# First-layer weights of an expert slot loaded in two transfers of 4 KB rows instead of one of 8 KB rows

## What is computed

```python
aff = x @ centroids.T
assign = jnp.argmax(aff, axis=1)
...
for e in range(nE):
    h = _layernorm(xs, ln_g[e], ln_b[e])
    h = jax.nn.relu(h @ w1[e].T + b1[e])
    ye = xs + h @ w2[e].T + b2[e]
    y = y + jnp.where((es == e)[:, None], ye, 0.0)
out_sorted = alpha * y + (1.0 - alpha) * xs
```

## The kernel before

| line | what |
|---|---|
| L771, L812 | tensor engine's wait for first weights |
| L780, L816 | layer 1 of a full, of a mixed slot |
| L799, L832 | layer 2 of a full, of a mixed slot |
| L2165 | the transfer that the change splits |

## Time and profile before

### The profile page before, as it was taken

One profiled execution on the slowest core, in us unless ns is written; L12 is line 12 of the kernel. 1 busy time (PEld: TensorE's weight loads), 2 busy tenths in 40 slices (PEclk: granted clock), 3 DMA queues, 4 the chain that ended last, 5 costly groups with the idle time before them and its releaser, 6 DMA issues.

```text
span 830.1 us, 19760 instructions
## 1 busy us (share of the span) xinstructions
PE 809.3 (97%) x7474; PEld 549.3 (66%) x7474; DVE 531.5 (64%) x1515; ACT 342.3 (41%) x574; POOL 281.4 (34%) x393
## 2 busy tenths in 40 slices
PE   8999999999999999999999999999999999999994
PEld 5655475476466557558547636859989976777673
DVE  5564368767757856866787755624579556566572
ACT  2444415513522541641541452232323275657660
POOL 3505011431512413223143160415454545443532
PEclk9999999999999999999999999999999999999998
DMA  7710300220030020040030033324543888978940
GB/s 255 221 49 26 77 1 1 65 66 1 27 103 1 27 53 1 2 128 2 1 97 9 1 103 129 108 66 164 190 148 134 301 318 305 323 268 315 345 201 17
DMA packets 63956, 96.47 MB, mean 116 GB/s; under 512 B 39347, under 2 KB 52276, under 8 KB 55926
## 3 DMA queue, kind: packets, MB, share of 16 engines
q1 hardware_dynamic: 58566, 83.56, 30.1%
q0 software_dynamic: 4864, 11.10, 4.3%
q10 hardware_dynamic: 432, 0.54, 0.2%
HBM read 84.22 MB, written 11.23 MB: 115 GB/s over the span
## 4 chain that ended last, share of the span: by engine, by line
PE 70%; DVE 17%; issue 5%; ACT 5%; POOL 1%; DMA 1%; another core or an unknown queue 0%; DVEq 0%; SPq 0%; ACTq 0%; POOLq 0%
PE ps L678 11%; PE ps L780 10%; PE ps L799 10%; PE ps L672 7%; PE ps L611 6%; PE ps L635 6%; PE ps L816 4%; PE ps L832 4%; DVE w_sb L1162 3%; PE ps L643 3%; PE ps L484 3%; DVE x3x L1162 3%; ACT arena L1662 2%; DVE st_ln L958 2%; DVE arena L1092 2%
## 5 line engine op out<-in xcount | busy, mean ns | idle before, releaser
L678 PE MATMUL ps<-ff2T,hT 128*128 128x256 f32 x512 | 121.6, 385 | 0.2 <-ACT hT L1654 0.2
L672 PE MATMUL ps<-x3x,ff1T 128*128 128x512 f32 x256 | 118.2, 605 | 0.1
L1662 ACT ACTIVATE arena<-ps 128x1536 f32<-128x1536 f32 (+3 forms) x49 | 65.1, 1328 | 113.3 <-DVE arena L1092 113.3
L678 PEld LDWEIGHTS ps<-ff2T,hT 128*128 128x128 f32 x512 | 94.3, 190 | 21.0 <-issue 8.1
L799 PE MATMUL ps<-w_sb,arena 128*128 x400 | 95.6, 382 | 0.0
L1880 POOL TENSOR_TENSOR rs_ln<-mv_ln,eps 128x4 f32<-128x4 f32 x24 | 4.9, 204 | 263.7 <-DVE mv_ln L965 263.7
L672 PEld LDWEIGHTS ps<-x3x,ff1T 128*128 128x128 f32 x256 | 46.0, 189 | 59.0 <-issue 50.9
L799 PEld LDWEIGHTS ps<-w_sb,arena 128*128 128x128 f32 x400 | 72.2, 190 | 12.2 <-issue 4.3
L611 PE MATMUL ps<-arena 32*128 32x512 f32 (+7 forms) x896 | 73.0, 434 | 3.1 <-ACT hT L1111 1.4
L1092 DVE SCALAR_TENSOR_TENSOR arena<-ps,arena 128x512 f32<-128x512 f32 (+4 forms) x59 | 45.0, 771 | 47.8 <-PE ps L635 28.8
L611 PEld LDWEIGHTS ps<-arena 32*128 32x128 f32 x896 | 36.0, 184 | 37.4 <-issue 17.9
(11 more groups left out here) (240 smaller groups left out, 1519.8 us busy)
## 6 DMA issues: line engine op xcount, KB each, us to landing
arena<-in_w SPq DMA_DIRECT2D x27, 1024.0 KB
hT<-in_w SPq DMA_DIRECT2D x16, 1024.0 KB
wts<-in_w SPq DMA_DIRECT2D x9, 1024.0 KB
w_sb<-in_w SPq DMA_DIRECT2D x8, 1024.0 KB, 5.4
token_store<-x SPq DMA_DIRECT2D x8, 520.0 KB, 3.4
arena<-in_x SPq DMA_DIRECT2D x7, 512.0 KB, 3.8
w_sb<-in_x SPq DMA_DIRECT2D x48, 64.0 KB, 2.4
arena<-in_epack SPq DMA_DIRECT2D x18, 134.0 KB
```

The costliest lines, as they stand in the source:

```text
L672: last = eng.matmul(ps[:, 6 + m % 2, :], ff1T[:, kd, m * P:(m + 1) * P], xT3[:, kd, :], start=kd == 0, stop=kd == KD - 1)
L678: last = eng.matmul(quarter(6, t), hT[:, m, t * P:(t + 1) * P], ff2T[:, m, :], start=m == 0, stop=m == FM - 1)
L1662: eng.activation(o, i, ACT.Relu).then_inc(s_sa, 1)
```

## The change

Each transfer of first weights becomes two: the columns of the first half of the contraction, then those of the second, 128 rows of 4 KB each. Both add 16 to the same semaphore, so the count that the tensor engine waits for doubles; it still waits for both halves before its first matmul of the part.

```diff
@@ -395,7 +395,7 @@
             for u in w1_of[j]:
                 used.setdefault(u, []).append(j)
-            turn_w1[j] = [16 * len(used[u]) for u in w1_of[j]]
+            turn_w1[j] = [16 * KD * len(used[u]) for u in w1_of[j]]
@@ -2162,7 +2162,9 @@
-                eng.dma_start(w1_ring[u], w1[bass.ds(at[p], P), :]).then_inc(s_w1[u], 16)
+                for kd in range(KD):
+                    c = slice(kd * FF, (kd + 1) * FF)
+                    eng.dma_start(w1_ring[u][:, c], w1[bass.ds(at[p], P), c]).then_inc(s_w1[u], 16)
```

## The result

The changed kernel takes 836.99 us (835.62 to 837.88, 6 runs) where the kernel before takes 832.46 (6 runs): a ratio of 1.0059, 95% interval 1.0044 to 1.0074. It is 4.5 us slower. A second series on another chip gave 1.0064 (1.0050 to 1.0078). The forecast was 832.9, no change, in a range to 836.0; the measured time is the small end of the rival in which the SP queue becomes the bound.

A forecast was written before the change was run, and what follows sets the result against it. TensorE was taken as the bound, with weights early. Rows of 4 KB 0, SP issues 0 and late list +0.35 us on the median 832.57 gave 832.9, no change; range 830.8 to 836.0.

The forecast's parts named there:

- the rival in which the SP queue becomes the bound: SP queue: added issues are held, over 0.9 us each SP no longer catches up; 836 to 838, or 855; chance 0.12.
- TensorE as the bound, weights early: Expert slots: TensorE busy 809.3 of 830.1 us, never waiting for a DMA; weights land 5 to 8 us early at the tightest.
- Rows of 4 KB: First-weights transfers: twice the rows add 0.06 us per transfer, 3 us of DMA time, hidden behind matmuls; counted 0.
- 52 issues on SP: SP's queue: 52 more issues at 0.52 us, 27 us over 315 us, absorbed by SP's waits; counted 0.
- the one tight place: SP at slot 28's two issues from 757.36: 2.08 us added against 1.48 of wait, so SP falls 0.6 us behind.
- catches up in the next pair: SP after the tightest pair: recovers its 0.6 us in the next, where the mean wait has 1.5 us to spare.
- that sign of being wrong: Issues of the weights' transfers on SP: many over 1 us would show the forecast wrong.
- The rival's small end: SP queue: half the added issues held, 4.1 us a pair, repeated late lists; 836 to 838; most of the rival's 0.12.
- Late list: Slot 31's token list and gather come 1.2 us later, delaying slot 29's turning; TensorE loses 0.35 us, between 0 and 1.7.
- since no lists are left to issue: Slot 31 and later: SP is idle again there, so no further loss from late lists was charged.
- I found no other turning so tight: Mixed-slot stretch: only slot 29's turning, with 0.86 us free, was found so tight and dependent on a list.
- A fixed latency paid in series: DMA queue: each extra transfer opens a 2.4 us gap, 892 (about 879 at the skill's 2.0 us); chance 0.02.

The follow-up runs named there:

- rows alone: Kernel before with each first-weights transfer still one transfer, but of 256 rows of 4 KB (halves apart in DRAM): 1.0002 of before.
- The two kernels with tiny DMAs, on one chip: Kernel before plus a tiny DMA, addressed from the weights' register, behind each first-weights transfer: 1.0042; the same with weights in rows of 4 KB: 1.0058.
- Tiny DMAs: Kernel before plus a DMA of 16 rows of 8 bytes behind each first-weights transfer: 1.0043; addressed from weights' register: 1.0042; that with 4 KB rows: 1.0058.
- tiny DMAs (weights' register): Kernel before plus a tiny DMA behind each first-weights transfer, its address taken from the weights' register: 1.0042 of before.
- four transfers for each: Four transfers with rows of 2 KB for each first-weights transfer of the kernel before, 156 issues more: 1.0464 of before, 38.6 us over.
- the kernel with partition halves: Two transfers for each of the kernel before, cut by partitions (64 partitions, rows of 8 KB): 1.0517 of before, times from 862 to 881 us.

## Why the prediction was wrong

**TensorE as the bound, weights early: right before, not after.** The lead of the weights, 5 to 8 us, was as read. It was taken as slack against one delay; SP's delay is carried from pair to pair, until TensorE waited for weights too, 0.8 and 0.9 us. (The DMA engines are busy, with digits 8 and 9, from slice 32 on, about 643 us, and not from slice 27; nothing hangs on that.)

**Rows of 4 KB: small, and 2 to 4 times undersized.** +0.06 us per transfer was forecast, with 0.12 as the bound. By the page the queue's packets took 31.4% of 836.1 against 30.1% of 830.1, 12.7 us more over 52 transfers, 0.24 each; with rows alone (31.3% of a span of 822.6, on another chip) 7.6 us, 0.15 each. The two kernels with tiny DMAs, on one chip, give 0.13 (30.9% of 833.1 against 30.1% of 832.2). The line through two points took undisturbed stretches (its slope is 39.6 ns per KB and not 38.7; the 7 ns per row stay); why rows cost more in the full stretch was not tried. That this hides was right as long as SP has waits: 1.0002 alone.

**52 issues on SP: the step that failed.** The sum has "SP issues 0": 52 more issues at 0.52 us were to fit into SP's waits, and SP was to catch up after the one tight place. Both sides of that balance were off.

The price came out at 0.69 and 0.78. The 0.85 us for two in a row, on which 0.52 stood, is this row of SP's timeline before:

```profile
741.15 0.85 SPq L2165 DMA_DIRECT2D arena<-in_w  x2
```

That pair was issued without a hold. Where SP issues without waits, runs of four issues take now 1.72 us (744.94), now 2.42 (762.52). Tiny DMAs cost 0.56 and 0.60, near the forecast, and 0.72 beside rows of 4 KB. Few single issues were long: 4 of 104 took over 1 us (one of 52 before, the 1.74), so that sign of being wrong did not show, while SP's waits were gone and TensorE waited at L816.

The waits were "25.0 us in seven waits, 3.6 each", set against four issues a pair. But the seven waits do not stand one to a pair. They stand in slots 17, 19, 24, 26, 28, 30 and 32, with 5.2, 3.5, 6.6, 1.7, 1.5, 2.4 and 4.1 us; the mixed slots 15 and 22 have none. From slot 15 on it is 25.0 us against 37 issues, so the room was 0.68 us for each, and not the 0.9 at which the rival was to begin. At 0.52 the 37 issues would have taken 19 of these 25 us; at 0.78 they take 29, and SP has no wait left. And SP "catches up in the next pair, where the mean wait has 1.5 to spare", says the text: that pair (slot 30) has 2.4 us of wait against 2.08, so 0.3 to spare.

What this does can be estimated by carrying the delay from slot to slot with the waits above, from the 2.15 us at slot 15 (656.17 against 654.02). With 0.78 the list of slot 31 comes 5.5 us late (measured 5.2), with 0.69 3.0 (measured 2.7 in the second series), with the forecast's 0.52 some 1.5. But the price is not the whole miss: the two kernels with tiny DMAs, at 0.56 and 0.60, still lose 3.1 and 3.5 us and not 0.35. What a late list costs was too small as well (next part).

The rival's small end, 836 to 838, was the result, and its chance of 0.12 was too low. That it hit is partly luck, since it had half of the added issues held for 1.74 us, and that did not happen.

**Late list: right place, wrong size.** The gather of slot 31 was to come 1.2 us later and cost TensorE 0.35. GpSimd's timeline of the changed kernel:

```profile
774.84 0.99 POOL L1959 DMA_INDIRECT arena<-token_store,ids  x1 [7.69 <-DMA ids<-slot_table]
```

It came 3.8 us later, with its list issued 5.2 us later (765.70 against 760.45), and the turning of slot 29 waited 0.71 us. And it was not the one place. The turnings of slots 27 and 31 waited longer, 1.55 and 1.60 us; with tiny DMAs (weights' register) those of slots 29 and 31 waited 1.0 us each. Slot 31 was held to be safe, "since no lists are left to issue", but its turning stands behind the gather of slot 33, whose list came 7.4 us later (783.32 against 775.96). "I found no other turning so tight" was true: before, L1391 of slot 31 ended 2.2 us ahead of its turning and that of slot 27 4.2 us, against 0.9 for slot 29. It does not help when the delay is larger than all three.

**The other rivals.** A fixed latency paid in series (892) is out: four transfers for each would have been far over the 38.6 us measured. The Trainium skill's rule against DMAs under 1 MiB (DMA: Bandwidth & Descriptors, Rules for kernel authors) gives the right sign here, but through the issuing queue's time and not the bandwidth: the smaller transfers cost nothing visible where SP had waits (1.0004 with 25 of them split). The 2.0 us that the prediction takes from that page of the Trainium skill stand in its section on a DMA issued by GpSimd (Anatomy of one DMA), and the transfers here are issued by SP; no run here shows them as a cost in series.

## What to carry to other kernels

Count a DMA queue's sequencer as an engine: sum its work between two of its waits, issues, table loads and all, and compare this with the period of the loop, place by place. Take the price of an issue where the queue is loaded, not from a pair in a quiet place. A mean over its waits is no slack, and a lead of lists or weights pays a delay once, not one that recurs each turn. When the queue's waits vanish from the profile, reordering its work only chooses which wait appears.

## What was not expected of the hardware

Transfers to 64 partitions with 8 KB rows ran at 236 GB/s with full DMA engines, against 350 for 128 partitions, and their issues took 0.47 us instead of 0.33. An issue with 256 rows of 4 KB took 0.38 us instead of 0.33. In the kernel with partition halves the granted clock of the stretch above is 0.91 of 2.4 GHz on the mean, so part of it lies at the lower level; there TensorE is busy for 15.6 of 20 us, and the kernel before, busy throughout, has 1.00 in all stretches shown.
